# Later four tiles' transposes in one go, projections in tile order, and two pieces of gate's low part ahead of the third tile's normalisation

## What is computed

```python
xn = _layernorm(x)
q = einsum('bse,edh->bsdh', xn, Wq) + bq        # 16 x 32 heads
k, v = the same with Wk, Wv                     # 16 x 8 heads, each repeated 4 times
attn = softmax(einsum('bsdh,bseh->bsde', q, k) / sqrt(16))    # 16 x 16 within a token
s = einsum('bsde,bseh->bsdh', attn, v)          # back to 512 features
nx = xn * rsqrt(mean(xn ** 2) + 1e-5) * ln_w
g = silu(down @ (silu(gate @ nx) * (up @ nx)))  # 1792 hidden features
out = x + s * g
```

## Time and profile before

| | |
|---|---|
| time, median of 3 runs (lowest to highest) | 472.58 us (472.14 to 472.69) |
| the profiled execution | 472.32 us, span 470.5 us |
| PE busy | 465.0 us, 99% of the span, 2134 instructions |
| PEld busy | 392.0 us, 83% |
| DVE busy | 412.7 us, 88% |
| ACT busy | 244.8 us, 52% |
| POOL busy | 122.4 us, 26% |
| chain that ended last, by engine | PE 97%, DMA 1%, DVE 1% |

### The profile page before, as it was taken

The page is one execution under the profiler, slowest core; times in us unless marked ns, Lnnn a source line. Parts: engine busy times, 40 slices in busy tenths (PEclk is TensorE's granted clock), DMA queues, the critical chain, the costliest instruction groups (busy, mean ns, idle before and its releaser), DMA issues.

```text
span 470.5 us, 6241 instructions
## 1 busy us (share of the span) xinstructions
PE 465.0 (99%) x2134; PEld 392.0 (83%) x2134; DVE 412.7 (88%) x559; ACT 244.8 (52%) x418; POOL 122.4 (26%) x105
## 2 busy tenths in 40 slices
PE   8999999999999999999999999999999999999997
PEld 7998888888888888888888888888888888888886
DVE  6999688987898898999979898999999888888994
ACT  5794665658688888654122545325235235358002
POOL 3931213216222112144352111110001111127920
PEclk9999999999999999999999999999999999999999
DMA  8707987669689975564374759555556655513762
GB/s 261 265 4 273 348 358 269 260 256 283 145 272 308 380 303 242 173 246 155 118 259 145 237 188 355 196 195 219 214 202 224 224 201 202 201 46 134 282 255 89
DMA packets 44623, 105.70 MB, mean 225 GB/s; under 512 B 20272, under 2 KB 21808, under 8 KB 41264
## 3 DMA queue, kind: packets, MB, share of 16 engines
q1 hardware_dynamic: 44592, 105.31, 62.9%
HBM read 69.90 MB, written 35.40 MB: 224 GB/s over the span
## 4 chain that ended last, share of the span: by engine, by line
PE 97%; DMA 1%; DVE 1%; POOL 0%; SPq 0%; issue 0%; ACT 0%; DVEq 0%; POOLq 0%
PE gu_ps L571 18%; PE gu_ps L568 18%; PE gu_ps L570 18%; PE y_ps L715 8%; PE y_ps L714 8%; PE y_ps L713 8%; PE gu_ps L715 3%; PE gu_ps L714 3%; PE gu_ps L713 3%; PE gu_ps L745 2%; PE gu_ps L744 2%; PE gu_ps L749 2%; DMA xz<-x 1%; PE y_ps L760 1%; PE gu_ps L588 0%; PE gu_ps L589 0%
## 5 line engine op out<-in xcount | busy, mean ns | idle before, releaser
L571 PE MATMUL gu_ps<-z_hi,w_ops 128*128 128x512 f32 x378 | 147.1, 389 | 0.0
L570 PE MATMUL gu_ps<-z_lo,w_ops 128*128 128x512 f32 x378 | 147.1, 389 | 0.0
L568 PE MATMUL gu_ps<-z_hi,w_ops 128*128 128x512 f32 x378 | 147.1, 389 | 0.0
L506 POOL TENSOR_TENSOR h_lo<-h,h_hi 128x512 fp32r<-128x512 f32 x28 | 37.1, 1324 | 228.5 <-ACT h_hi L956 228.4
L568 PEld LDWEIGHTS gu_ps<-z_hi,w_ops 128*128 128x128 f32 x378 | 71.0, 188 | 14.8
L571 PEld LDWEIGHTS gu_ps<-z_hi,w_ops 128*128 128x128 f32 x378 | 70.9, 188 | 14.7
L570 PEld LDWEIGHTS gu_ps<-z_lo,w_ops 128*128 128x128 f32 x378 | 70.9, 188 | 14.7
L715 PE MATMUL y_ps<-wd_ops,h_lo 128*128 128x512 f32 x168 | 65.5, 390 | 0.0
L714 PE MATMUL y_ps<-wd_ops,h_hi 128*128 128x512 f32 x168 | 65.5, 390 | 0.0
L713 PE MATMUL y_ps<-wd_ops,h_hi 128*128 128x512 f32 x168 | 65.4, 390 | 0.0
L956 ACT ACTIVATE h_hi<-h 128x512 fp32r<-128x512 f32 x28 | 17.7, 631 | 58.9 <-DVE h L1260 58.9
(11 more groups left out here) (146 smaller groups left out, 753.1 us busy)
## 6 DMA issues: line engine op xcount, KB each, us to landing
w_kept<-w_ops SPq DMA_DIRECT2D x13, 1792.0 KB, 7.6
w_ops<-w_kept SPq DMA_DIRECT2D x13, 1792.0 KB, 7.3
wd_ops<-wd_kept SPq DMA_DIRECT2D x35, 512.0 KB, 3.8
raw<-gate_up SPq DMA_DIRECT2D x30, 256.0 KB, 3.9
wd_kept<-wd_ops SPq DMA_DIRECT2D x14, 512.0 KB, 8.0
xz<-x SPq DMA_DIRECT2D x16, 256.0 KB, 5.6
raw<-down SPq DMA_DIRECT2D x14, 256.0 KB, 3.9
w_ops<-wd_kept SPq DMA_DIRECT2D x7, 512.0 KB, 7.1
```

What stands on the lines that cost most here:

```text
L506: pool.tensor_tensor(lo, src, hi.bitcast(F32), ALU.subtract).then_inc(h_lo_done, 1)
L568: pe.matmul(acc, w_h, z_hi[:, zi, c, :], start=start and c == 0, stop=False, skip_group_check=True)
L570: pe.matmul(acc, w_h, z_lo[:, zi, c, :], start=False, stop=False, skip_group_check=True)
L571: end = pe.matmul(acc, w_l, z_hi[:, zi, c, :], start=False, stop=c == 1, skip_group_check=True)
```

## The change

- DVE makes two of the four pieces of gate's low part between the normalisations of the second and the third tile (tiles 1 and 2), not one. The semaphore that ACT raises for it comes after its second piece (`gate_hi_two`, formerly `gate_hi_one` after its first).
- The variance for the rms of the first four tiles (`x_variance(0)`) goes behind both low parts, and the projection weights' low halves (`lo_qkv`) go from behind the statistics of tile 4 to ahead of them.
- PE: product 2 goes ahead of the transposes of tiles 4 and 5, and those of all four later tiles come in one go behind it.
- The products of the first pair are issued by tile, 0 to 7: tile 3 is fourth, not eighth. `QKV_ORDER` goes.
- ACT normalises all four later tiles ahead of their first high part, instead of in between.
- DVE: the low parts of the later four tiles go behind the take of product 2, instead of in between the takes.
- `t_hi(0, 3)` waits for all eight products instead of seven.

No instruction is added or removed except waits; the arithmetic is the same.

```diff
--- before.py
+++ after.py
@@ -62,7 +62,6 @@
     JJ = 2 * J
     WARM_UP = 32
     SLOTS = 13
-    QKV_ORDER = ((0, 1, 2, 4, 5, 6, 7, 3), (0, 1, 2, 3, 4, 5, 6, 7))
     GATE_BANK, UP_BANK = 1, 2
     LAST = GROUPS - 1
 
@@ -171,7 +170,7 @@
         h_hi_done, wd_hi_done = sem("h_hi_done"), sem("wd_hi_done")
         gu_scaled, w_hi_a, w_hi_s = sem("gu_scaled"), sem("w_hi_a"), sem("w_hi_s")
         z_shift_done, mean_done, z_act_done = sem("z_shift_done"), sem("mean_done"), sem("z_act_done")
-        mean0_done, z_shift0_done, z_act0_done, gate_hi_one = sem("mean0_done"), sem("z_shift0_done"), sem("z_act0_done"), sem("gate_hi_one")
+        mean0_done, z_shift0_done, z_act0_done, gate_hi_two = sem("mean0_done"), sem("z_shift0_done"), sem("z_act0_done"), sem("gate_hi_two")
         z_hi_done, z_raw_done, t_hi_done = sem("z_hi_done"), sem("z_raw_done"), sem("t_hi_done")
         wqkv_hi_done, exp_done, y_done, table_loaded = sem("wqkv_hi_done"), sem("exp_done"), sem("y_done"), sem("table_loaded")
 
@@ -239,7 +238,7 @@
             return w_late[:, u - LATE] if u >= LATE else wd_ops[:, u % 3]
 
         def qkv_index(tile):
-            return JJ * (tile // JJ) + QKV_ORDER[tile // JJ].index(tile % JJ)
+            return tile
 
         def parts(f, j):
 
@@ -721,8 +720,7 @@
                     down_tile(u, j)
 
             def qkv_product(index):
-                pair = index // JJ
-                j = QKV_ORDER[pair][index % JJ]
+                pair, j = divmod(index, JJ)
                 if pair:
                     pe.wait_ge(z2_lo_done, 2 * (j // J) + 2)
                 else:
@@ -772,11 +770,9 @@
             first_products()
             qkv_product(0)
             qkv_product(1)
-            second_tile(J)
-            second_tile(J + 1)
             qkv_product(2)
-            second_tile(J + 2)
-            second_tile(J + 3)
+            for j in range(J, JJ):
+                second_tile(j)
             qkv_product(3)
             qkv_product(4)
             gate1(0)
@@ -839,8 +835,8 @@
                 for n, (m, c, k) in enumerate(first_places(part)):
                     end = act.activation(w_ops[:, 0, 0, m, c * P:(c + 1) * P], gu_raw[:, 0, 2 * m + c, :], ACT.Copy,
                                          scale=lnw_sb[:, k:k + 1])
-                    if part == n == 0:
-                        end.then_inc(gate_hi_one, 1)
+                    if part == 0 and n == 1:
+                        end.then_inc(gate_hi_two, 1)
                 end.then_inc(w_hi_a, 1)
 
             def hi_a(n):
@@ -906,7 +902,7 @@
                 act.wait_ge(t_added, 4 * pair + n + 1)
                 if zi == ZT4:
 
-                    act.wait_ge(qkv_done, JJ * (pair + 1) - (pair == 0))
+                    act.wait_ge(qkv_done, JJ * (pair + 1))
                     act.wait_ge(m3_done, NI if pair else 1)
                 act.activation(z_hi[:, zi, :, :], zT[pair][:, k:k + 2, b * TB:(b + 1) * TB], ACT.Copy).then_inc(t_hi_done, 1)
 
@@ -1007,10 +1003,10 @@
             z_tile(J)
             z_tile(J + 1)
             hi_wd(0)
+            z_tile(J + 2)
+            z_tile(J + 3)
             z_hi_tile(J)
-            z_tile(J + 2)
             z_hi_tile(J + 1)
-            z_tile(J + 3)
             z_raw_tile(J)
             z_hi_tile(J + 2)
             z_raw_tile(J + 1)
@@ -1208,8 +1204,8 @@
                 dve.tensor_tensor(w_sum[:, 3, :], a12, w_sum[:, 1, :], ALU.subtract).then_inc(w_summed, 1)
 
             def first_lo(part, places=slice(0, K)):
-                if (part, places.stop) == (0, 1):
-                    dve.wait_ge(gate_hi_one, 1)
+                if (part, places.stop) == (0, K // 2):
+                    dve.wait_ge(gate_hi_two, 1)
                 else:
                     dve.wait_ge(w_hi_a, part + 1)
                 for m, c, k in first_places(part)[places]:
@@ -1234,7 +1230,7 @@
                                   ALU.subtract).then_inc(w_lo_s, 1)
 
             def qkv_take(index):
-                tile = JJ * (index // JJ) + QKV_ORDER[index // JJ][index % JJ]
+                tile = index
                 bank = qkv_bank(index)
                 assert tile < SLOTS or taken[0] >= values_end(tile - SLOTS)
                 dve.wait_ge(qkv_done, index + 1)
@@ -1351,31 +1347,28 @@
                 if j == 0:
                     dve.tensor_scalar(minus_mean0[:], mean_var[:, 0, 0:1], -1.0, None, ALU.mult).then_inc(mean0_done, 1)
             normalise_tile(1)
-            first_lo(0, slice(0, 1))
+            first_lo(0, slice(0, K // 2))
             normalise_tile(2)
             normalise_tile(3)
-            first_lo(0, slice(1, K))
-            x_variance(0)
+            first_lo(0, slice(K // 2, K))
             for j in range(J):
                 z_lo_tile(j)
             first_lo(1)
+            x_variance(0)
+            lo_qkv(0)
+            lo_qkv(1)
             for j in range(J, JJ):
                 stats_tile(j)
                 aggregate(j)
                 variance(j)
                 mean_of(j)
-                if j == J:
-                    lo_qkv(0)
-                    lo_qkv(1)
             x_variance(J)
             qkv_take(0)
-            z_lo_tile(J)
             qkv_take(1)
-            z_lo_tile(J + 1)
             times_up0(0)
             qkv_take(2)
-            z_lo_tile(J + 2)
-            z_lo_tile(J + 3)
+            for j in range(J, JJ):
+                z_lo_tile(j)
             qkv_take(3)
             t_add(0, 0)
             t_add(0, 1)
```

## The result

The changed kernel takes 473.62 us in the median of 13 runs (472.93 to 474.61) beside 472.50 us for the kernel before on the same chips (13 runs, 471.91 to 472.80): a ratio of 1.0027, 95% interval 1.0019 to 1.0035, so 0.9 to 1.65 us slower. The difference of the two medians is 1.12 us, the ratio alone gives 1.28. The forecast was 473.7 us, 1.1 above the median before.

The account below looks back on a forecast made before the run. The tensor engine, busy throughout from 10.30 to 465.00 us, was taken to bound the kernel. Its nested waits of 0.26, 0.9 and 1.11 us made 1.11, added to the median 472.58: 473.7 us, range 472.8 to 474.3.

Parts of the forecast that it names:

- The sum: Whole kernel: nested tensor engine waits of 0.26, then 0.9, then 1.11 us, not added up, so 1.11 us slower.
- Two pieces: Vector engine ahead of the third tile's normalisation: two pieces wait for the second activation, putting normalisation off 0.33 us.
- Weights' low halves: Projection weights on the vector engine: halves done 0.9 us earlier, so four matmuls lose their 0.07 us delay.
- The variance: Variance moved behind the low parts: GpSimd's scales come later, but the last normalisation has 0.45 us cover, costing nothing.
- rival C: Vector engine and GpSimd collide once more, another 1.1 us, giving 474.8 us; chance 0.07.
- Four transposes in one go: Tensor engine, later tiles: joining gains below 0.1 us, but tile 4's first transpose starts at 22.68 instead of 20.33.
- Chain from z_hi(4) to t_add(0, 0): Alternating scalar and vector copies: z_hi(4) at 23.31, t_add(0, 0) at 28.11 instead of 27.00, vector engine 1.11 us late.
- Takes, m1(1), m7(1): Tensor engine stands about 0.35 us at product 6 and again at m1(1); at m7(1) the 1.11 goes in whole.
- The rule on the port: Two-input vector instructions and GpSimd's SBUF reads exclude each other: 1.1 us of the three t_adds' 4.71, kept unchanged.
- Rival A: The h_lo collision at the t_adds falls away, leaving the tensor engine only 0.26 late: 472.8 us; chance 0.12.
- Rival D: Tensor engine's clock falls to its lower level for sixteen transposes and product 3: 3.5 us more, 477.2; chance 0.02.

Follow-up runs that it names:

- e2: Changed kernel with one piece of gate's low part again, not two, ahead of the third tile's normalisation: 473.68 us, ratio 1.0021.
- e5: Changed kernel with the first four tiles' variance back ahead of their low parts and h_lo(0) behind the third t_add: 473.56 us, ratio 1.0030.
- e3: Changed kernel with the variance of the first four tiles back ahead of their low parts: 473.25 us, ratio 1.0018.
- e4: Changed kernel with GpSimd's h_lo(0) made only after the third t_add: 474.01 us, ratio 1.0036.
- e9: Changed kernel with h_lo(0) behind t_add(0, 3), variance ahead of the low parts, one piece ahead of the third normalisation: 472.45 us, ratio 1.0003.
- e10: Kernel before with three added sums over the bias on the vector engine ahead of t_add(0, 0), as padding: 472.65 us, ratio 1.0008.
- e8: Changed kernel with GpSimd's h_lo(0) put behind t_add(0, 3): 472.50 us, ratio 1.0006.
- e6: Changed kernel with variance ahead of the low parts, h_lo(0) behind the third t_add, one piece ahead of the third normalisation: 473.31 us, ratio 1.0020.

## Why the prediction came out right, step by step

- **Median and direction.** 473.7 forecast, 473.62 measured. The sum behind it was 1.11; the rows say 0.17 ahead of R in both profiles of the changed kernel (0.11 to 0.53 with two pieces in general) and 1.16 to 1.28 behind it, 1.3 to 1.5. The timing (1.1 by medians, 1.28 by the ratio, interval 0.9 to 1.65) doesn't tell these apart. Ahead of R the sum had 0.33 and got 0.17; behind R it had 1.11 - 0.33 = 0.78 and got 1.16 to 1.28, for a reason of its own, below. The two misses go opposite ways, so that the medians meet the forecast within 0.1 us is partly luck; the direction and most of the chain are not.
- **Two pieces: 0.33 forecast, 0.11 to 0.53 measured.** The arithmetic was right for the execution it was read from. There the scalar engine's first activation of the gate had waited for a DMA and started 0.58 us behind the aggregate of tile 3; in the changed kernel's profile it starts 8.69 - 8.27 = 0.42 behind, and the cost is 0.17. The step that was missed is that this start hangs on a load that varies from execution to execution, so the term is a range and not a number. That it lies on the path is shown as far as R. Behind R the path goes over the vector engine, whose start doesn't follow the tensor engine's there; that a saving at R would be lost again in the gap ahead of product 6 is argued from these waits, and e2 agrees without deciding it.
- **Weights' low halves: right.** Four matmuls now take 19.26 - 18.57 = 0.69 us (0.76 before).
- **The variance, "cover 0.45 us, so nothing": wrong.** This is the one step whose mechanism failed. I bounded the last normalisation by its old time, although the same sentence said that GpSimd starts later; what GpSimd would then run beside, I priced only in rival C. I also compared with the wrong reader: z_hi(4) stands behind that normalisation on the scalar engine and was planned for 23.31, so even the old end, 23.54, was too late for it, by 0.23 less the 0.1 that instructions overlap. There was no cover. GpSimd then met the two instructions on the weights' low halves, was held 1.5 us, the last normalisation started 23.88 - 8.27 = 15.61 behind the aggregate (22.74 - 7.35 = 15.39 before; 14.76 in e5, with the variance early), and z_hi(4) came at 24.60 - 10.54 = 14.06 behind R instead of the forecast 23.31 - 9.79 = 13.52. That is 0.54 us on the vector engine's path, and 0.4 to 0.5 in the tensor engine's loss (e3, and e4 to e5). Rival C was this in kind, but gave it a chance of 0.07 and 1.1 us.
- **Four transposes in one go: right.** Tile 4's transpose was forecast at 22.68 - 9.79 = 12.89 behind R and came at 12.89; the joining is worth nothing (e9).
- **Chain from z_hi(4) to t_add(0, 0): right.** Forecast 28.11 - 23.31 = 4.80 us, measured 29.39 - 24.60 = 4.79.
- **Takes, m1(1), m7(1): mechanism right, sizes up by what GpSimd added.** Forecast were waits of about 0.35 us at product 6 and again at m1(1). From the matmul before it to its own start, product 6 loses 0.64 us and m1(1) another 0.22, each with 0.08 more to its second matmul; at m7(1) the weight load waits 0.27 and costs 0.10. That is 1.12 of the 1.16. The forecast carried the lateness at t_add(0, 0) on whole; of the measured 1.31 there, 1.19 arrives at t_add(0, 3). The waits contain one another, as said, and behind t_add(0, 3) the chain has no slack (e10: 0.50 in, 0.46 out).
- **The rule on the port.** I kept the t_adds at 4.71; they took 4.72. The Trainium skill (SBUF — State Buffer, "Who interferes with whom") says that a vector instruction with two SBUF inputs and a GpSimd instruction reading SBUF exclude each other for a whole instruction. The runs agree for h_lo: 1.10 us is charged to whichever vector instruction with two SBUF inputs is next (second t_add 2.32, first sum 1.52). In e10, where most of h_lo runs beside the sums of the bias, with one input, only 0.23 is charged, to the first t_add, which met h_lo's end. Rival A, that the collision falls away, didn't happen by itself; e8 makes it happen; forecast was 0.26 us over the kernel before, and it is 0.25 over it (interval -0.1 to 0.7).
- **Rival D didn't happen.** The granted clock reads 1.00 for the changed kernel, but it also reads 1.00 from 1.6 to 6.5 us in the kernel before, where the transposes are 0.213 us apart and not 0.109, so the pace is the better witness: product 3 takes 27.41 - 25.22 = 2.19 us behind sixteen transposes and took 26.27 - 24.08 = 2.19 behind eight. The forecast's reading of the start was right: in the kernel before the last of the 32 first transposes are already 0.109 apart, ahead of any other matmul.

## What to carry to other kernels

An engine that is busy for 88% of the span can still have no slack in one chain: read the slack where the engine that bounds the kernel waits for it, by ends and starts. When a step moves ahead of another on the same engine, compare its end with the start of that next step, and not only with the need of an engine further on. When a step on GpSimd is moved, ask which vector instruction with two SBUF inputs it now runs beside, since in these runs one of the two waited; a collision can be moved behind the last wait that matters, but an edit that only shifts it to the next such instruction gains nothing. Compare profiles of a kernel with varying load times from a mark behind the loads, and where a term hangs on a load's arrival, give it a range.

## What was not expected of the hardware

GpSimd's instruction, asked for 0.17 us behind the first of two back-to-back vector instructions of 0.94 us each, was not let in between them: it took 2.52 us, five times out of five. In the kernel before, GpSimd's short instructions that began in the middle of the same two took 0.58 and 1.27 instead of 0.20 and 0.56, and h_lo got in between two t_adds and held the second for 1.1 us. With the variance early (e3, e5, e6, e9) the instruction that met the two, again a power on four columns, asked for 0.4 us behind the first, took 1.41 to 1.42 instead of 1.01. Why a GpSimd instruction gets in between in one case and not in the other no run here settles. The loads' arrival moved the aggregate of tile 3 by up to 1.5 us between profiled executions, more than the whole effect (1.1 to 1.3), while the medians of the kernel before in four series lie between 472.25 and 472.50.
